# Layer 1's W2 turned by VectorE's 32x32 transposes and a DRAM exchange, its Hadamard product in a bank of its own

## What is computed

```python
def fwht(x):                      # Walsh-Hadamard along the last axis, 1/sqrt(n)
    while h < n:
        xb = x.reshape(-1, n // (2 * h), 2, h)
        a, b = xb[:, :, 0, :], xb[:, :, 1, :]
        x = jnp.stack([a + b, a - b], axis=2).reshape(-1, n)
        h *= 2
...
hidden = jax.nn.silu(einsum('bsd,hd->bsh', x, W1)) * einsum('bsd,hd->bsh', x, W3)
hidden = fwht(hidden)
out = jnp.einsum('bsh,dh->bsd', hidden, W2)
...
x = x + s * _silu(_L1_ffn_ref(xn, W1, W2, W3))
```

## Time and profile before

| | us |
|---|---|
| median of 3 runs | 365.25 (365.09 to 366.41) |
| the profiled execution | 365.77 |
| its span, first to last instruction | 364.0 |
| PE busy | 356.7 |
| DVE busy | 250.2 |
| ACT busy | 165.6 |
| POOL busy | 102.0 |

### The profile page before, as it was taken

How to read it: one execution, slowest core, us unless ns; L and a number is a source line. 1 busy time by engine, 2 the same in 40 slices (tenths; PEclk the granted TensorE clock), 3 DMA queues, 4 the chain that set the end, 5 groups by cost and what they waited for, 6 DMA issues and landing times.

```text
span 364.0 us, 5036 instructions
## 1 busy us (share of the span) xinstructions
PE 356.7 (98%) x1817; PEld 302.2 (83%) x1817; DVE 250.2 (69%) x479; ACT 165.6 (45%) x327; POOL 102.0 (28%) x128
## 2 busy tenths in 40 slices
PE   6999999999999999999999999999999999999996
PEld 3888888887888888888888878888888888888895
DVE  5579965888469846977558894688636887356632
ACT  2645371354243624454284644645446454454501
POOL 1142700146114641555707030060300603004002
PEclk9899999999999999999999999999999999999999
DMA  7996110433334543431143401433305342054001
GB/s 229 290 298 220 59 59 0 146 87 108 95 116 138 169 129 115 120 115 29 59 131 74 146 0 44 148 72 106 100 14 175 72 125 80 0 189 112 19 2 58
DMA packets 42337, 38.63 MB, mean 106 GB/s; under 512 B 5701, under 2 KB 41801, under 8 KB 42313
## 3 DMA queue, kind: packets, MB, share of 16 engines
q1 hardware_dynamic: 42312, 38.32, 34.8%
HBM read 24.09 MB, written 14.22 MB: 105 GB/s over the span
## 4 chain that ended last, share of the span: by engine, by line
PE 96%; DMA 1%; DVE 1%; SPq 1%; issue 0%; ACT 0%; DVEq 0%
PE GU L357 20%; PE GU L359 20%; PE GU L358 20%; PE O L357 8%; PE O L358 8%; PE O L359 8%; DMA stage<-in_L_ffn_W 1%; PE T L364 1%; PE O L364 1%; PE O L428 1%; PE T L357 1%; PE T L359 1%; PE T L358 1%; PE O L501 1%; PE O L500 1%; PE O L499 1%
## 5 line engine op out<-in xcount | busy, mean ns | idle before, releaser
L696 ACT ACTIVATE hf<-GU 128x512 f32<-128x512 f32 x64 | 38.2, 599 | 85.1 <-DVE hid L809 59.7
L945 DVE TENSOR_TENSOR hf<-hf,GU 128x512 f32<-128x512 f32 x64 | 43.5, 680 | 31.2 <-PE GU L359 25.5
L357 PE MATMUL GU<-XT,W1T 128*128 128x512 f32 x128 | 50.9, 397 | 0.0
L809 DVE TENSOR_TENSOR hid<-hf,hid 128x512 fp32r<-128x512 f32 x64 | 49.6, 774 | 1.2 <-ACT hid L632 0.8
L359 PE MATMUL GU<-XT,W1T 128*128 128x512 f32 x128 | 49.9, 390 | 0.0
L358 PE MATMUL GU<-XT,W1T 128*128 128x512 f32 x128 | 49.9, 390 | 0.0
L357 PE MATMUL GU<-XT,W3T 128*128 128x512 f32 x128 | 49.9, 390 | 0.0
L359 PE MATMUL GU<-XT,W3T 128*128 128x512 f32 x128 | 49.8, 389 | 0.0
L358 PE MATMUL GU<-XT,W3T 128*128 128x512 f32 x128 | 49.8, 389 | 0.0
L357 PE MATMUL O<-hid,W2hi 128*128 128x512 f32 x112 | 44.0, 393 | 0.0
L358 PE MATMUL O<-hid,W2hi 128*128 128x512 f32 x112 | 43.7, 390 | 0.0
(11 more groups left out here) (187 smaller groups left out, 737.5 us busy)
## 6 DMA issues: line engine op xcount, KB each, us to landing
stage<-in_L_ffn_W SPq DMA_DIRECT2D x24, 256.0 KB, 5.4
swap_rows<-GX SPq DMA_DIRECT2D x7, 512.0 KB, 3.5
sT<-swap_rows SPq DMA_DIRECT2D x28, 128.0 KB, 2.7
swap_gate<-GX SPq DMA_DIRECT2D x7, 512.0 KB, 2.9
sT<-swap_gate SPq DMA_DIRECT2D x28, 128.0 KB, 2.6
swap_p<-PX SPq DMA_DIRECT2D x4, 640.0 KB, 3.2
PL<-swap_p SPq DMA_DIRECT2D x16, 160.0 KB, 3.3
swap_w<-GX SPq DMA_DIRECT2D x4, 512.0 KB, 2.9
```

What stands on the lines that cost most here:

```text
L357: pe.matmul(o, lhs(0), rhs(0), start=start, stop=False)
L696: act.activation(hf[:, c % 2, :], GU[:, c % 2, 0, :], ACT.Silu).then_inc(silu_done, 1)
L809: dve.tensor_tensor(dst, src, hi_part.bitcast(F32), ALU.subtract).then_inc(done, 1)
L945: dve.tensor_tensor(hf[:, c % 2, :], hf[:, c % 2, :], GU[:, c % 2, 1, :], ALU.mult).then_inc(mul_done, 1)
```

## The change

W2 of layer 1 takes the road of W1 and W3. VectorE turns its 32x32 blocks into a new tile BX (`b_turn`), SyncE writes BX to DRAM (`scatter_b`) and reads it back into the slot's W2 part (`gather_b`), ScalarE makes the high part in two pieces (`w2_landed_hi`), GpSimd the low part in two pieces (`w2_landed_lo`, VectorE made it before). The sixteen transposes on TensorE go. The Hadamard product is written to T[:, i % 2] in place of O[:, 1], and stands behind the last up chunk (pairs 0, 2, 3) or behind up chunk 2 of group two (pair 1). The scaling into U moves to the next group: after chunk 0 and chunk 3 of group two, after chunk 0 of group three, and for the last pair into n = 4. The butterflies move with it. SyncE's `move_w` is split in two, and the scatter of W2 stands between the scatter and the gathers of W1/W3. The reload of a slot waits for W2's low part in place of its transposes.

```diff
@@ SyncE, for n in 1..3
                 move_gate(n - 1)
-                for j in ((0,), (1, 2), (3,))[n - 1]:
-                    move_w(PAIRS + j)
+                scatter_w(PAIRS + (0, 1, 3)[n - 1])
+                scatter_b(PAIRS + (0, 2, 3)[n - 1])
+                gather_w(PAIRS + (0, 1, 3)[n - 1])
+                gather_b(PAIRS + (0, 2, 3)[n - 1])
+                if n == 1:
+                    scatter_b(PAIRS + 1)
+                    gather_b(PAIRS + 1)
+                if n == 2:
+                    scatter_w(PAIRS + 2)
+                    gather_w(PAIRS + 2)
...
-                    sp.wait_ge(w2_tr, PAIRS + n)
+                    sp.wait_ge(w2_lo_part, 2 * n)
@@ SyncE, new
+            def scatter_b(i):
+                sp.wait_ge(b_turned, i - PAIRS + 1)
+                if i > PAIRS:
+                    sp.wait_ge(b_moved, 64 * (i - PAIRS))
+                sp.dma_start(swap_b.rearrange("j p f -> p j f"), BX[:, :, :]).then_inc(b_out, 16)
+            def gather_b(i):
+                sp.wait_ge(b_out, 16 * (i - PAIRS) + 16)
+                for j in range(QUADS):
+                    sp.dma_start(w2_slot(i)[j * Q:(j + 1) * Q], swap_b[j].rearrange("(q b) f -> b q f", q=QUADS)).then_inc(b_moved, 16)
@@ TensorE
             def next_hadamard(i):
-                pe.wait_ge(u_ready, i)
-                pair_hadamard(i, w2nat)
+                pe.wait_ge(w2_lo_part, 2 * (i - PAIRS) + 2)
+                pe.wait_ge(u_ready, i - 1)
+                for e in (0, 1):
+                    last = pe.matmul(T[:, i % 2, :], hadmR[:, :], w2nat[:, e, :, :].rearrange("p a d -> p (a d)"), start=(e == 0), stop=(e == 1))
+                last.then_inc(h_done, 1)
...
             def block0_group(n):
...
                 for c in range(HC):
                     up_chunk(0, n, c, False)
-                    if c == 2:
-                        pe.wait_ge(gateT_ready, 2 * n)
-                        next_pair_w2(PAIRS + (0, 2, 3)[n - 1])
-                    if c == 4:
-                        next_hadamard(PAIRS + (0, 2, 3)[n - 1])
-                        if n == 1:
-                            next_pair_w2(PAIRS + 1)
-                    if c == 6 and n == 1:
+                    if c == 2 and n == 2:
                         next_hadamard(PAIRS + 1)
+                next_hadamard(PAIRS + (0, 2, 3)[n - 1])
                 recurrent_mix(n)
@@ ScalarE, new, called after chunk 0 of n = 2 (pair 1) and chunk 6 (pairs 0, 2, 3)
+            def w2_landed_hi(i):
+                act.wait_ge(b_moved, 64 * (i - PAIRS) + 64)
+                act.wait_ge(h_done, i)
+                for c in (0, 1):
+                    act.activation(w2_part(0, c), w2_landed(i, c), ACT.Copy).then_inc(w2_hi_part, 1)
@@ VectorE, between_chunks
                 if n < NB:
+                    if c == 0 and n > 1:
+                        j = (0, 2)[n - 2]
+                        pair_u(1, PAIRS + j, j)
                     if c == 1:
                         w_turn(PAIRS + (0, 1, 3)[n - 1], n)
-                    if c == 3:
-                        nat_lo(PAIRS + (0, 2, 3)[n - 1], w2nat)
-                        if n == 2:
-                            w_turn(PAIRS + 2, n)
-                    if c == 5:
-                        j = (0, 2, 3)[n - 1]
-                        pair_u(1, PAIRS + j, j)
-                        if n == 1:
-                            nat_lo(PAIRS + 1, w2nat)
-                    if c == 7 and n == 1:
+                        b_turn(PAIRS + (0, 2, 3)[n - 1])
+                    if c == 3 and n == 1:
+                        b_turn(PAIRS + 1)
+                    if c == 3 and n == 2:
                         pair_u(1, PAIRS + 1, 1)
+                        w_turn(PAIRS + 2, n)
@@ GpSimd, block0_group
                 rms_of(n - 1)
+                if n == 2:
+                    w2_landed_lo(PAIRS + 1)
                 rstd_of(n + 1)
...
-                for j in ((0,), (1, 2), (3,))[n - 1]:
-                    landed_lo(PAIRS + j)
-                for j in ((0, 1), (2,), (3,))[n - 1]:
-                    pair_butterfly(1, j, PAIRS + j + 1)
+                landed_lo(PAIRS + (0, 1, 3)[n - 1])
+                if n == 2:
+                    pair_butterfly(1, 0, PAIRS + 1)
+                    pair_butterfly(1, 1, PAIRS + 2)
+                if n == 3:
+                    pair_butterfly(1, 2, PAIRS + 3)
+                w2_landed_lo(PAIRS + (0, 2, 3)[n - 1])
+                if n == 2:
+                    landed_lo(PAIRS + 2)
```

More of the change, by code:

```diff
@@ L139, in two_block_kernel @@
         PZ = sb("PZ", [P, 2 * P + BLOCKS * P])[:, 0:BLOCKS * P]
+        with ExitStack() as early:
+            BX = sb("BX", [P, QUADS, 4 * Q], F32, early)
         c2B = sb("c2B", [P, ROWS])
@@ L162, in slot_of, with w2_slot, w2_landed, w2_part @@
             return stage[:, i % 2, 0:2, :].rearrange("p w f -> p (w f)").rearrange("p (q f) -> p q f", q=QUADS)
+        def w2_slot(i):
+            return stage[:, i % 2, 2, :].rearrange("p (q f) -> p q f", q=QUADS)
+        def w2_landed(i, c):
+            return w2_slot(i).rearrange("p q (a c b) -> p q a c b", a=2, c=2)[:, :, :, c, :].rearrange("p q a b -> p a q b")
+        def w2_part(e, c):
+            return w2nat[:, e, c, :].rearrange("p (a q b) -> p a q b", a=2, q=QUADS)
         def w_landed(i, w, k):
@@ L548, in block0_group @@
             def block0_group(n):
-                pe.wait_ge(u_ready, PAIRS + (0, 2, 3)[n - 1])
+                if n == 1:
+                    pe.wait_ge(u_ready, PAIRS)
                 for i in range(HC):
@@ L580, in block1_group @@
                 pe.wait_ge(mul_done, 8 * n)
+                if prev_layer == 0:
+                    pe.wait_ge(u_ready, 2 * PAIRS)
                 for i in range(TILES):
@@ L747, in block0_group @@
                     chunk(n, c, False)
-                    if c == 3:
-                        nat_hi(PAIRS + (0, 2, 3)[n - 1], w2nat)
-                    if c == 5 and n == 1:
-                        nat_hi(PAIRS + 1, w2nat)
+                    if c == 0 and n == 2:
+                        w2_landed_hi(PAIRS + 1)
+                    if c == 6:
+                        w2_landed_hi(PAIRS + (0, 2, 3)[n - 1])
                     if c == 5:
@@ L823, in pair_u @@
                 dve.wait_ge(h_done, i + 1)
-                dve.tensor_scalar(U[l][:, bass.ds(2 * j, 2), :].rearrange("p a d -> p (a d)"), O[:, 1, :], float(H) ** -0.5, None,
+                bank = O[:, 1, :] if l == 0 else T[:, i % 2, :]
+                dve.tensor_scalar(U[l][:, bass.ds(2 * j, 2), :].rearrange("p a d -> p (a d)"), bank, float(H) ** -0.5, None,
                                   ALU.mult).then_inc(u_ready, 1)
@@ L880, in first_x_lo, with b_turn @@
                     lo(xT[1][k], GU[:, 1, k, :], xT[0][k], xt_hi, k + 1, xt_ready)
+            def b_turn(i):
+                dve.wait_ge(stage_loaded[i % 2][2], 16 * (i // 2 + 1))
+                if i > PAIRS:
+                    dve.wait_ge(b_out, 16 * (i - PAIRS))
+                dve.transpose(BX[:, :, :].rearrange("p j (c b) -> p c j b", b=Q),
+                              stage[:, i % 2, 2, :].rearrange("p (c j a) -> p c j a", j=QUADS, a=Q)).then_inc(b_turned, 1)
             def w_turn(i, n):
@@ L1083, in block1_group @@
                     recurrent_scale(n - 1)
+                    pair_u(1, 2 * PAIRS - 1, PAIRS - 1)
                 else:
@@ L1175, in second_norm, with w2_landed_lo @@
                 pool.tensor_tensor(c2[:, 0:TILES], ctmp[:, :], mhalf[:, :], ALU.pow).then_inc(c2_ready, 1)
+            def w2_landed_lo(i):
+                for c in (0, 1):
+                    pool.wait_ge(w2_hi_part, 2 * (i - PAIRS) + c + 1)
+                    pool.tensor_tensor(w2_part(1, c), w2_landed(i, c), w2_part(0, c).bitcast(F32), ALU.subtract).then_inc(w2_lo_part, 1)
             def landed_lo(i):
```

12 lines of the change are left out of this document (5 added, 7 removed).

## The result

| | before | after |
|---|---|---|
| median of 6 runs each, us | 365.88 (365.09 to 366.41) | 374.44 (373.52 to 376.0) |
| the profiled execution | 365.77 | 373.86 |
| its span | 364.0 | 372.1 |
| ratio after to before, 95% interval | | 1.0241 (1.0214 to 1.0267) |

The change makes the kernel 8.6 us slower. The direction was forecast (+4.2 us); the size lies above the range, which ended at 371.8.

What follows compares the result with a forecast made beforehand. TensorE, busy 98% of the span, was taken as the bound. Groups one, two and three gave -1.9 + 4.9 + 1.2 = +4.2 us (3.0 to 5.9) on a 365.25 median: 369.5 us, range 367.6 to 371.8.

Steps and rivals of the forecast that it cites:

- where it would wait: Before the last Hadamard product of each group, TensorE waits for GpSimd's w2nat: at most 0.5, about 4.8 and 1.6 us.
- a sign of being wrong: Time going outside the three windows, each from a group's first up-projection matmul to its first mix matmul.
- Removed work: On TensorE, four transpose blocks (1.76 us) and a 0.75 us wait in group one go: 2.5 us gain without other waits.
- The covers: On SyncE's queue, W2's transfers hide; W1/W3 gathers start about +12.4 in group two and land before ScalarE wants them at +18.4.
- rival 4: W1/W3 gathers through DRAM land 1 to 2 us late and ScalarE holds its queue: 370.5 to 371.5 us, chance 0.06.
- VectorE's term in group two: VectorE's net added 1.0 us puts the low part of hid chunk 3 at +16.68; GpSimd's W1/W3 low parts end at +22.24.
- rival 1: Behind group two's 4.8 us idle stretch the clock falls to 1.2 GHz, costing 1.6 us: 371.1 us, chance 0.25.
- The second step that failed: Group three: W2's low part late behind one pair of butterflies, mix at +24.05, 1.2 us more (1.0 to 1.8).
- Group two: W2's low part waits behind four butterfly halves (3.5 us) and takes 1.45: mix at +27.75, 4.9 us more (4.2 to 5.6).
- Group one: W2's low parts take 1.65 us and end at +22.1: mix at +22.65, 1.9 us less (2.2 to 1.5).
- The 0.6 a collision: VectorE and GpSimd fighting for SBUF: the skill's rule gives 0.6 us each, about 0.5 more in all; 0.45 was used.
- Rivals 2 and 3: Whole kernel: 2, all stalls vanish, 362.8 us, chance 0.08; 3, a smaller stall, 367.4 us, chance 0.15.

Runs made afterwards that it cites:

- the last experiment: Changed kernel with W2 first on all four queues, W1/W3 low parts of pair 2 moved to group three, c2 turned after chunk 2 there: 362.79 us, 0.9915 of before.
- the kernel without the exchange: Changed kernel without W2's scatter and gathers through DRAM, high and low parts reading the slot as loaded: 375.11 us, 1.0245 of before.
- the kernel without the turns: Changed kernel without VectorE's four W2 turns, SyncE scattering the slot as loaded: 372.43 us, 1.0167 of before.
- one moved line: Changed kernel with W2's low part ahead of the pair butterflies on GpSimd, nothing else: 366.45 us, 1.0015 of before.
- W2 first: Changed kernel with W2 ahead of W1 and W3 on VectorE, SyncE, ScalarE and GpSimd, butterflies behind both: 364.23 us, 0.9961 of before.
- bank alone: Kernel before with only layer 1's Hadamard products written to T[:, i % 2], W2 staying on TensorE: 365.70 us, 0.9995 of before.

## Why the prediction was right or wrong

**What bounds the kernel, and where it would wait: right.** TensorE's order was the bound, the wait stands where it was forecast, behind the eight up chunks of groups two and three, and it names GpSimd's w2nat. Its length was forecast as 4.8 and 1.6 us, and at most 0.5 in group one; it is 5.05, 2.67 and 0.47. **Where the time would go: wrong in part.** Of the 8.8 us, 2.2 lie outside the three windows, in the stretches right behind two of them, which the prediction itself had named as a sign of being wrong.

**Removed work: somewhat too small.** At most 2.5 us were said to be there to win, with all stalls gone; the last experiment wins 3.1. By the prediction's terms its windows would be 2.18 and 0.44 shorter in groups one and three and 0.11 longer in group two; they are 2.33, 0.52 and 0.14 shorter. Its group two, which holds two Hadamard products, took 22.67, against 22.21 and 22.31 with one: in a dense stream a product costs 0.36 to 0.46 rather than 0.55.

**The covers: right.** SyncE's queue of after in group two: W1/W3 scatter and W1/W3 gathers; the W2 scatter goes out between them, at 108.06.

```profile
107.46 0.38 SPq L259 DMA_DIRECT2D swap_w<-GX  x1
...
110.88 1.75 SPq L302 DMA_DIRECT2D stage<-swap_w  x4
```

The W1/W3 gathers go out at 110.88, +12.06 (+12.4 was forecast), 3.4 after their scatter, as in the earlier trace rows. Taking W2's transfers away changed nothing, so rival 4 was no danger.

**VectorE's term in group two: close.** Low part of hid chunk 3 at 115.16, +16.34 (+16.68); GpSimd's W1/W3 low parts end at 120.67, +21.85 (+22.24). In group one the same end is at +20.45 (+20.42).

**The step that failed: the clock.** The sum priced what a wait does to the work behind it at nothing, and put the clock into rival 1, with a chance of 0.25, for group two alone, at 1.6 us. It fell twice. By the trace it costs 1.33 us in group two and 1.51 in group three, 2.84 in all; putting matmuls into the waits gave back 2.4. What was weighed against it was wrong: it held that at the start the transposes counted, and that a matmul stream on both sides would protect. In the groups there were such streams on both sides, and it fell all the same. That the groups before showed no fall was no evidence, since their idle times were 0.6 us at most. The Trainium skill, TensorE: Matmul & The Clock Gate, "What's actually happening", which the prediction named beside this rival, has the lower clock come back with idleness; the trace agrees, with 0.50 behind idle times of 5.05 and 2.67 us. But a fall doesn't follow on every such wait: in the profile of the kernel without the exchange none came behind the same 2.67 us. Of the six waits of 2 us or more in three kernels, five brought one, among them all three of group two, for which the prediction had given a chance of 0.25.

**The second step that failed: group three, 1.1 us too short without the clock.** Without the clock the window is 2.3 longer than before, above the bound of 1.8. VectorE's low part of hid chunk 3 comes at 157.23, +15.33, not +14.85. VectorE's timeline of after, group three, shows what was left out:

```profile
156.63 0.69 DVE L995 TENSOR_TENSOR hf<-hf,GU 128x512 f32<-128x512 f32 x1 [0.72 <-ACT hf L737]
157.23 0.68 DVE L850 TENSOR_TENSOR hid<-hf,hid 128x512 fp32r<-128x512 f32 x1
```

ScalarE's Silu of chunk 4 (start 156.00) waits for VectorE's low part of chunk 2, and VectorE's multiply of chunk 4 waits for that Silu. The prediction had subtracted group two's extra work from VectorE's column as if nothing else could hold it; without that work it runs into a wait of 0.72, and 0.5 us come back. The other 0.6 are collisions: the two butterfly halves took 1.83 (1.45), the W2 low part 1.90 to the start of TensorE (1.65).

The butterfly halves on GpSimd in group three of after:

```profile
162.76 1.18 POOL L1188 TENSOR_TENSOR U<-U 128x256 f32<-128x256 f32 x1
163.90 0.72 POOL L1189 TENSOR_TENSOR U<-U 128x256 f32<-128x256 f32 x1
```

**Group two, 0.3 too short without the clock.** Earlier low parts (-0.4) were more than used up by the butterflies (3.64, not 3.5) and W2's low part, which took 1.93 instead of 1.45. It was held that two collisions in the butterflies would spend them; a third low part of hid stood beside W2's. **Group one, 0.3 too short:** its W2 low part took 1.93, not 1.65. In this kernel the pieces came out at or near the upper bound each time, so that the upper bound of each would have been the better forecast; in the kernel without the turns the four halves took 3.21. The 0.6 a collision that the prediction set against its 0.45 took the whole of the other instruction as lost. What was lost here was about what was left of it, 0.14 to 0.5 us, so that neither figure holds for every collision.

The rise was 8.6 us where 4.2 were forecast. Of the 4.4 that are missing, the clock is about 2.4 to 2.8, group three 1.1, groups one and two 0.3 each. The clock alone doesn't account for the miss: with it held up by matmuls the rise is still 6.1 us (372.01), just above the sum's upper bound of 5.9. Rivals 2 and 3, a faster or barely slower kernel, did not occur as the change stands; the no-wait state of rival 2 was reached once W2 went first everywhere, not by a faster engine but by another order.

## What to carry to other kernels

When work moves from the bounding engine to a chain through others, write down for each queue on the chain what stands ahead of the piece that is waited for, and put that piece first: one moved line was worth 8.0 us here, the whole reorder 11.6. A wait that leaves TensorE idle for 2 us or more in a dense stream may cost a fall of its clock too: of six such waits in three kernels, four cost 1.3 to 1.5 us more, one 2.6 and one nothing. Where two engines may collide, take the upper of the two durations, and after taking work off an engine ask what it waits for next.

## What the runs showed of the hardware

- The granted clock went to 0.50 behind idle times of 5.05, 3.97, 2.67 and 2.10 us in a dense matmul stream, for 3.4 us, and behind 5.05 us in the kernel without the exchange for 6.8. It stayed at 1.00 behind 2.67 us in that same kernel, and behind 1.36, 0.96, 0.86 and 0.55 in others. In the kernel with 2.10 us the Hadamard product right behind the wait still ran at full speed (0.73), and the fall came after TensorE had resumed.
- At the start of the kernel, where TensorE idles before its first transposes, the length of the idle time doesn't decide it: a fall followed behind 1.52 (W2's low part ahead), 1.64 (matmuls in the wait), 1.66 (before) and 1.77 us (the last kernel), and none behind 1.38 (W2 first), 1.57 (bank alone) and 1.60 us (no turn).
- VectorE's low part of hid (both inputs in SBUF, 0.68 us alone) and GpSimd's operations on 128x256 (0.73 alone) held each other up, each by about what was left of the other's when it started. In group two of after, VectorE's at 122.59 took 1.18 beside a butterfly half that ran from 122.49, and the next half, from 123.17, took 1.17; the one at 120.44, shortly before the end of a GpSimd low part, took only 0.82. VectorE's multiply at 121.98, with one input in the bank GU, and the half beside it took 0.69 and 0.73, as alone.
- A broadcast issued 1.1 us before a scatter to DRAM went with 4.8 us until the gathers behind the scatter (5.1 in after); issued 4.0 us before it, with 2.9. The distance isn't all of it: in the attention groups of before, 2.2 to 2.9 us ahead, the scatter took 3.6 to 4.8.
